# A Flamingo block on one core: k copied by VectorE, attention rows normalised by GpSimd, and a feed-forward that begins with half steps

## What is computed

```python
query = einsum("bnc,dc->bnd", ctx, Wq) + bq        # ctx: 4 x 256 x 128, f32
key = einsum("bnc,dc->bnd", ctx, Wk) + bk
attention = softmax(query @ key^T, axis=-1)        # 4 x 256 x 256
x = x + tanh(g_xattn) * einsum("bln,bmn->blm", layernorm(x), attention)
h = layernorm(x)                                   # then fp8
act = gelu(h @ w_gating[0]) * (h @ w_gating[1])    # 256 -> 1024, fp8 products
x = x + tanh(g_ffn) * (act @ w_linear)             # 1024 -> 256
```

## Time and profile before

| | |
|---|---|
| median of three runs | 50.8 us (50.74 to 51.58) |
| the profiled execution | 50.57 us |
| its span, first to last instruction | 48.8 us |
| TensorE busy | 42.9 us, 88% |
| VectorE busy | 35.7 us, 73% |
| ScalarE busy | 29.5 us, 60% |
| GpSimd busy | 16.9 us, 35% |

### The profile page before, as it was taken

The page is one execution under the profiler, slowest core; times in us unless marked ns, Lnnn a source line. Parts: engine busy times, 40 slices in busy tenths (PEclk is TensorE's granted clock), DMA queues, the critical chain, the costliest instruction groups (busy, mean ns, idle before and its releaser), DMA issues.

```text
span 48.8 us, 842 instructions
## 1 busy us (share of the span) xinstructions
PE 42.9 (88%) x245; PEld 29.6 (61%) x245; DVE 35.7 (73%) x111; ACT 29.5 (60%) x67; POOL 16.9 (35%) x35
## 2 busy tenths in 40 slices
PE   0999999995999999998999999999999999995300
PEld 0318788882887988863435655765656788872000
DVE  2101069999978979989999991887666998899910
ACT  4601643799799699844599749754446944662000
POOL 3205992009999823410510160000000697005000
PEclk9999999999999999999999999999999999999996
DMA  0495999999999991000000000000000025230083
GB/s 0 80 309 108 349 402 327 196 202 176 194 201 153 104 97 9 0 0 7 0 0 0 13 0 0 0 0 0 7 0 0 0 104 163 66 110 0 0 321 109
DMA packets 3460, 4.64 MB, mean 95 GB/s; under 512 B 384, under 2 KB 2048, under 8 KB 3456
## 3 DMA queue, kind: packets, MB, share of 16 engines
q1 hardware_dynamic: 2592, 3.80, 23.7%
q0 software_dynamic: 864, 0.79, 17.5%
HBM read 5.90 MB, written 1.05 MB: 142 GB/s over the span
## 4 chain that ended last, share of the span: by engine, by line
PE 64%; DVE 15%; DMA 9%; SPq 3%; ACT 2%; issue 1%; DVEq 1%
PE bank L627 15%; PE bank L633 14%; PE bank L652 14%; PE bank L587 14%; DMA x_sb<-x 9%; DVE st L403 6%; PE bank L559 4%; SPq L205 3%; DVE nmax L410 2%; PE bank L609 2%; DVE mv L406 2%; PE bank L552 2%; DVE aq L470 2%; DVE attn L421 1%; ACT xq L337 1%
## 5 line engine op out<-in xcount | busy, mean ns | idle before, releaser
L461 DVE SCALAR_TENSOR_TENSOR ap<-bank,gl 128x512 f16<-128x512 f32 (+1 forms) x20 | 11.6, 580 | 3.5 <-issue 1.6
L346 ACT ACTIVATE gl<-bank 128x512 bf16<-128x512 f32 (+1 forms) x20 | 10.0, 509 | 6.0 <-PE bank L627 6.0
L652 PE MATMUL bank<-wl,aq 128*128 128x256 fp8e4 x64 | 10.1, 273 | 0.7 <-DVE aq L470 0.6
L627 PE MATMUL bank<-xq,wg 128*128 128x512 fp8e4 (+1 forms) x40 | 10.2, 337 | 0.2 <-ACT xq L337 0.2
L633 PE MATMUL bank<-xq,wg 128*128 128x512 fp8e4 (+1 forms) x40 | 10.2, 337 | 0.0
L652 PEld LDWEIGHTS bank<-wl,aq 128*128 128x128 f16 x64 | 6.0, 98 | 4.1 <-DVE aq L470 1.6
L587 PE MATMUL bank<-attnT,xT_sb 128*128 128x256 f32 x32 | 8.1, 385 | 0.0
L470 DVE TENSOR_SCALAR aq<-ap 128x512 uint16<-128x512 uint16 (+1 forms) x20 | 6.6, 334 | 0.0
L270 POOL TENSOR_TENSOR yo<-ys,x 128x256 f32<-128x256 f32 x4 | 2.9, 750 | 9.3 <-ACT ys L354 9.3
L587 PEld LDWEIGHTS bank<-attnT,xT_sb 128*128 128x128 f32 x32 | 5.6, 190 | 0.7 <-ACT attnT L320 0.2
L255 POOL TENSOR_TENSOR r<-ve,neg_half 128x2 f32<-128x2 f32 x4 | 3.0, 760 | 8.5 <-DVE ve L444 8.5
(11 more groups left out here) (51 smaller groups left out, 55.9 us busy)
## 6 DMA issues: line engine op xcount, KB each, us to landing
x_sb<-x SPq DMA_DIRECT2D x4, 256.0 KB, 4.7
xT_sb<-xT SPq DMA_DIRECT2D x4, 256.0 KB, 8.5
out<-yo SPq DMA_DIRECT2D x6, 128.0 KB, 2.1
wg<-w_gating POOLq DMA_DIRECT2D x4, 128.0 KB, 10.1
par<-params_ctxT SPq DMA_DIRECT2D x1, 258.0 KB, 2.8
par<-params_ctxT SPq DMA_DIRECT2D x1, 256.0 KB, 4.2
wl<-w_linear POOLq DMA_DIRECT2D x2, 128.0 KB, 9.7
out<-yo SPq DMA_DIRECT2D x1, 256.0 KB, 2.0
```

Of the source, the lines that this page charges most:

```text
L346: nc.scalar.activation(gl[:, s % 2, toks], gate_b[s % 2][:, toks], ACT.Gelu_apprx_tanh).then_inc(gelu_ready, 1)
L461: nc.vector.scalar_tensor_tensor(ap[:, s % NAP, toks], up_b[s % 2][:, toks], ACT_SCALE, gl[:, s % 2, toks], ALU.mult, ALU.mult).then_inc(p ...
L627: mm = nc.tensor.matmul(gate_b[s % 2][:, toks], wg8[:, c, k, 0, o:o + P], xq[:, g, k, toks], start=(k == 0), stop=(k == KC - 1))
L652: mm = nc.tensor.matmul(halves(y_b[g][i])[:, t], aq[:, s % NAQ, m:m + P], wl8[:, j], start=(j == 0 and t == 0), stop=(j == HT - 1), skip_g ...
```

## The change

Four things move. VectorE copies k out of PSUM in place of ScalarE. GpSimd normalises the rows of all four sequences, and VectorE none. VectorE's program is reordered: stats1 of one sequence stands after each copy of k instead of three of them standing at the front. TensorE transposes the attention rows and xh tile by tile, with a wait for each tile of 128 rows, and its order of attend parts and of energy(0) and project_k(1) is shifted. The first two hidden slices of group 0 are made as half steps, sequence 0 first (two steps), then sequence 1 (two steps), which makes 22 steps of what were 20, with X_AFTER moved accordingly; turn_x2(1) now stands behind the two half steps of sequence 0.

```diff
-    STEPS = [divmod(n, HT) + (0, GB) for n in range(G * HT - SPLIT)]
+    FIRST = 2
+
+
+    STEPS = [(0, j, i, i + 1) for i in range(GB) for j in range(FIRST)]
+    STEPS += [divmod(n, HT) + (0, GB) for n in range(FIRST, G * HT - SPLIT)]
     STEPS += [(G - 1, j, i, i + 1) for i in range(GB) for j in range(HT - SPLIT, HT)]
     S = len(STEPS)
-    X_AFTER = (3, 6)
+    X_AFTER = (5, 8)
...
+            normalise(0)
+            normalise(1)
             scales1()
             shift_x(0)
+            normalise(2)
             shift_x(1)
-            normalise(B - 1)
+            normalise(3)
...
-            def k_out(b):
-                act.wait_ge(k_done, b + 1)
-                nc.scalar.activation(kT[:, b * L:(b + 1) * L], k_b[b % 2][:, 0:L], ACT.Identity,
-                                     bias=bk).then_inc(k_ready, 1)
...
             q_out(0)
-            k_out(0)
             q_out(1)
-            k_out(1)
             q_out(2)
-            k_out(2)
             exps(0)
             q_out(3)
-            k_out(3)
             exps(1)
             attn_out(0)
             exps(2)
+            attn_out(1)
             exps(3)
-            attn_out(1)
             attn_out(2)
...
+            def k_out(b):
+                dve.wait_ge(k_done, b + 1)
+                if b == 0:
+                    dve.wait_ge(s_ctx[0], 16)
+                nc.vector.tensor_scalar(kT[:, b * L:(b + 1) * L], k_b[b % 2][:, 0:L], bk, None,
+                                        ALU.add).then_inc(k_ready, 1)
...
-            def normalise(b):
-                invert_sum(b)
-                dve.wait_ge(rsum_ready, b + 1)
-                for t in range(LT):
-                    nc.vector.tensor_scalar(attn[:, b, t], e[:, b, t], rsum[:, b, t:t + 1], None,
-                                            ALU.mult).then_inc(attn_ready, 1)
...
-            for b in range(B - 1):
-                stats1(b)
+            k_out(0)
+            stats1(0)
             row_max(0)
-            stats1(B - 1)
+            k_out(1)
+            k_out(2)
+            stats1(1)
+            invert_sum(0)
             row_max(1)
-            normalise(0)
+            k_out(3)
+            stats1(2)
+            invert_sum(1)
             row_max(2)
-            normalise(1)
+            stats1(3)
             row_max(3)
-            normalise(2)
-            invert_sum(B - 1)
+            invert_sum(2)
+            invert_sum(3)
...
-                if b < B - 1:
-                    pe.wait_ge(attn_ready, LT * (b + 1))
-                else:
-                    pe.wait_ge(pool_attn_ready, LT)
...
-                turn(turn_b[b % 2], attn[:, b]).then_inc(attn_turned, 1)
+                for t in range(LT):
+                    pe.wait_ge(pool_attn_ready, LT * b + t + 1)
+                    for k in range(KC):
+                        mm = nc.tensor.transpose(halves(turn_b[b % 2])[:, k, t * P:(t + 1) * P],
+                                                 attn[:, b, t, k * P:(k + 1) * P], ident[:, :])
+                mm.then_inc(attn_turned, 1)
...
-                for k in range(KC):
-                    for t in range(LT):
+                for t in range(LT):
+                    if b < 2:
+                        pe.wait_ge(xh_ready, LT * b + t + 1)
+                    else:
+                        pe.wait_ge(act_xh_ready, LT * (b - 2) + t + 1)
+                    for k in range(KC):
...
-                    pe.wait_ge(xq_ready, GB * (g + 1))
+                    pe.wait_ge(xq_ready, GB * g + i1)
...
             project_k(0)
             project_q(1)
+            energy(0)
             project_k(1)
-            energy(0)
             project_q(2)
             project_k(2)
             energy(1)
...
             attend(0, [(0, 0), (0, 1)])
             turn_attention(1)
             attend(0, [(1, 0), (1, 1)])
+            attend(1, [(0, 0), (0, 1)])
             turn_attention(2)
-            attend(1)
+            attend(1, [(1, 0), (1, 1)])
+            attend(2, [(0, 0), (0, 1)])
             turn_attention(3)
-            attend(2)
+            attend(2, [(1, 0), (1, 1)])
             attend(3, [(0, 0), (0, 1)])
             turn_x2(0)
-            attend(3, [(1, 0)])
+            attend(3, [(1, 0), (1, 1)])
+            for s in range(FIRST):
+                ffn1(s)
             turn_x2(1)
-            attend(3, [(1, 1)])
             for s in range(S):
-                ffn1(s)
+                if s >= FIRST:
+                    ffn1(s)
                 if s >= LAG:
```

More of the change, by code:

```diff
@@ L157, in flamingo_block @@
         rsum_ready = sem("rsum_ready")
-        attn_ready = sem("attn_ready")
         pool_attn_ready = sem("pool_attn_ready")
@@ L192, in flamingo_block @@
         s_out = sem("s_out")
+        first_of_g1 = next(s for s, step in enumerate(STEPS) if step[0] == 1)
         def last_step(b):
@@ L388, in _ @@
                     xq_out(3)
-                if s == HT + LAG:
+                if s == first_of_g1 + LAG:
                     scale_out(0)
-                if s == HT + LAG + 1:
+                if s == first_of_g1 + LAG + 1:
                     scale_out(1)
@@ L554, in energy @@
                 mm.then_inc(energy_done, 1)
-            def turn(to, src):
-                for k in range(KC):
-                    for t in range(LT):
-                        mm = nc.tensor.transpose(halves(to)[:, k, t * P:(t + 1) * P],
-                                                 src[:, t, k * P:(k + 1) * P], ident[:, :])
-                return mm
             def turn_attention(b):
@@ L593, in turn_x2 @@
                 if b < 2:
-                    pe.wait_ge(xh_ready, LT * (b + 1))
-                else:
-                    pe.wait_ge(act_xh_ready, LT * (b - 1))
-                if b < 2:
                     pe.wait_ge(attnT_ready, B - 1 + b)
@@ L644, in ffn2 @@
                     pe.wait_ge(x2_ready, LT * B)
-                    pe.wait_ge(xq_ready, 2)
-                if s == HT:
+                if (g, j) == (0, 0):
+                    pe.wait_ge(xq_ready, i1)
+                if s == first_of_g1:
                     pe.wait_ge(xq_ready, B)
```

## The result

| | before | changed |
|---|---|---|
| median | 50.77 us (50.74 to 51.58, 4 runs) | 55.34 us (55.31 to 55.68, 4 runs) |
| ratio | | 1.090, 95% interval 1.085 to 1.095 |
| the profiled execution | 50.57 us | 55.35 us |
| its span | 48.8 us | 53.6 us |
| mean granted clock | 0.992 | 0.968 |

A forecast was written before the change was run, and what follows sets the result against it. TensorE was taken to bound the kernel: holes added, 2.85 + 0.24 + 0.5 + 1.1 + 0.18 + 0.24 = 5.1, less 1.42 removed, put 3.7 on 50.57, giving 54.3. Own range 53.0 to 54.9, overall 52.4 to 56.6.

The forecast's parts named there:

- The wait at turn_attention(2): On TensorE ahead of the third transposition: stands from 15.75 to 18.60 for GpSimd's rows of sequence 2, 2.85.
- the chain from the last statistics to the first xs: On GpSimd, from the last statistics to the first shifted x: takes 3.43 as before, of which the power is 1.68.
- three half blocks more: On TensorE ahead of turn_attention(2): listed as work without a wait, up to 15.75.
- Why scales1 is late: On GpSimd: it starts at 13.73 because VectorE's extra work makes the last statistics 3.1 late.
- second rival: VectorE's statistics complete by 11.2, so TensorE never stands at turn_attention(2): time 50.7, chance 0.10.
- first rival: Clock falls in TensorE's hole at turn_attention(2), delaying the feed-forward by 1.5 to 2.5: 55.8 to 56.8, chance 0.25.
- the forecast's hole of 0.5: On TensorE ahead of attend(3): waits for ScalarE's copy attnT(3) until 22.82, 0.5.
- The hole for gelu(0): On TensorE after sequence 0's half steps: waits for gelu(0) behind xq_out(1), 1.1, then product(0), 0.18.
- The wait for product(2): On TensorE in the feed-forward: product(2) stands behind sequence 3's second statistics on VectorE, 0.24.
- What was costed at nothing: Extra half steps, tile-wise waits, ScalarE's lost copies (1.9), VectorE's lost normalisations (2.3) and unmoved weight transfers: no effect on the time.
- The 0.45 that VectorE no longer loses: VectorE's normalisations beside GpSimd's xs: some 0.45 comes back, but VectorE is not waited for, so no gain.
- The sum: Whole kernel: 50.57 for the profiled execution and 3.7 of delay give 54.3.

The follow-up runs named there:

- e2: Changed kernel with stats1(3) ahead of row_max(2) on VectorE: 54.00 us, ratio 1.061.
- e11: Kernel before with only the rows moved: GpSimd normalises all four sequences in the changed kernel's order, ScalarE still copies k: 54.18 us, ratio 1.066.
- e9: Changed kernel with full steps from the start and stats1(3) ahead of row_max(2): 52.97 us, ratio 1.042.
- e1: Changed kernel with ten matmuls on zeros filling TensorE's hole ahead of turn_attention(2)'s wait for the rows: 54.23 us, ratio 1.070.
- e3: Changed kernel with GpSimd's normalise(2) ahead of scales1: 57.27 us.
- e4: Changed kernel with gelu(0) and gelu(1) ahead of xq_out(1) on ScalarE: 53.89 us, ratio 1.061.
- e5: Kernel before with only the half steps, turn_x2(1) behind the two of sequence 0: 51.77 us, ratio 1.022.
- e6: Changed kernel with full steps from the start and turn_x2(1) between the last quarters of attend(3), as before: 54.05 us.
- e7: Kernel before with only the transpositions of attention rows and xh tile by tile: 50.66 us, ratio 0.995.

## Why the prediction was right, and where it was not

**The wait at turn_attention(2).** Right, and close: statistics over at 13.64 (13.73 forecast), first shifted x at 16.82 (17.16), transposition at 18.37 (18.60). The copy of k on VectorE takes 0.48 and starts its successor after 0.40 (0.38 taken). A term that is off is the chain from the last statistics to the first xs, 3.18 instead of 3.43. TensorE is also through with the work ahead at 15.93 and not 15.75, so the hole is 2.44 from start to start, where the text had 2.85. Its list of that work is one half block too long ("three half blocks more"; with the block times given, 15.75 holds two, and two stand in the program), which did not enter the sum.

**Why scales1 is late.** Half right. In the changed kernel the row says that scales1 waited for the statistics, 0.53, and e2 gained that. But the text gave all of the delay to VectorE's extra work, and named statistics complete by 11.2 as the point from which TensorE never stands. e11 has them at 10.5, and the hole is 2.40. The rows of sequences 0 and 1 ahead of scales1, which wait for exps(1) in e11 and for the reciprocal behind stats1(2) in e2, hold it until 13.3 to 13.7 alone; VectorE's work holds it to about the same moment, so each hides the other. My second rival, "the statistics come in time", rested on a condition that does not suffice. In numbers: rows alone 54.2, copies of k alone 52.6, both 54.05 (full steps in all three). These are not pure differences: the kernel of the copies alone has stats1(3) early, and its partner in that is e9 with 52.97, so that there the rows on GpSimd add 0.4; and the kernel of the rows alone keeps TensorE's old order, with all of attend(1) behind the third transposition.

**The clock.** It was the first rival, with a chance of 0.25, that came true, not the forecast. I had priced it at 1.5 to 2.5 more; it cost 1.05 (e1). What I had right is that a part hides behind attnT(3): the forecast's hole of 0.5 there is missing in the changed kernel and is back, at 0.35, as soon as the clock stays up. The price was too high because I let every matmul of attend(1), attend(2) and turn_attention(3) behind the hole take twice its time, 2.9 more (3.0 by the text's own block times), and took off about 0.5 for what hides. The clock was low from 19.4 to 22.8 only: the first two matmuls of what was left of attend(1) and the last half block of attend(2), which starts at 22.86, ran at full rate. Against the filled hole the low clock added 1.6 (22.86, when the last half of attend(2) starts, is 9.05 behind scales1, against 21.44 or 7.46), and 0.54 of it hid behind attnT(3). This is the term that was mis-sized: with 1.05 instead of 1.5 to 2.5 the first rival gives 55.35, and 55.34 was measured. The measured time lies neither in the forecast's own range (53.0 to 54.9) nor in the first rival's (55.8 to 56.8), but between them; that it is inside 52.4 to 56.6 is owed to the width that the rival gave. The Trainium skill (TensorE: Matmul & The Clock Gate, Part 1) has the fall after idleness, which this trace agrees with, and e3 as well. The trace of e11, with a longer wait (2.40), has no fall.

**The hole for gelu(0).** Right: 1.05 and 0.26 (1.1 and 0.18 forecast). e4 shows that ScalarE's order is part of its cause: with gelu(0) ahead, 0.69 of the hole is left, for the transposition and the copy of sequence 1, which come late with the half steps. e5 shows the same 1.05 with the half steps alone, on the kernel before. The wait for product(2), 0.24 in the forecast, is 0.13. The prediction did not say outright that the half steps are a loss by themselves, though its own sum had it: 0.42 saved, about 1.5 added. e5 and e6 put it at 1.0 and 1.3.

**What was costed at nothing** stayed so. The tile-wise waits are worth 0.5% (e7). ScalarE's relief let exps(0) start at 8.69 instead of 9.86 and exps(1) at 10.79 instead of 11.48, but the third transposition waited for neither, and ScalarE waited more itself (5.1 for the transpositions, 0.8 before). The new places of energy(0), project_k(1) and the parts of attend were not run by themselves. The 0.45 that VectorE no longer loses beside GpSimd's xs is not waited for, as forecast.

**The sum.** Forecast 3.7 after 50.57; in the trace 4.8. Of the 1.1 between them the clock is 1.05.

## What to carry to other kernels

An engine with idle time is not free if its program has a shared step in it: ask what a new instruction ahead of that step waits for, because the step then waits for it too, and price that before moving it. Whether the rows of sequence 1 behind scales1 would have done better was not run. When two moves load the same chain, try each alone, since a single row names only what came last and hides the one that came just before. Smaller first steps start sooner, but they also cover less of the latency behind them; compare the matmul time that stands ahead of the first consumer with the time until its result is back.

## What the runs showed that I had not expected

In the changed kernel the clock did not fall in the hole but a microsecond behind it: TensorE was idle from 16.2 to 18.3 and resumed at full rate, the fall came at 19.4, and it took 3.4 us until the rate was back. A hole is thus not always paid for once it is over. The place of the fall is not fixed: it came 0.8 behind the resumption in e6, just at the resumption in e4 and within the hole of 3.14 in e3, and the clock stayed low for 3.4, 3.4 and 6.8.

Nor does the length of the hole alone decide, since the same kernel goes both ways. With a wait of 2.2 in the trace, the clock fell in all four executions of the changed kernel, in three of four of e6 and in one of four of e4; with 2.40 (e11) in one of four, and with 1.53 (e2, e9) in one of four each. What decides it no run here tells. So the 1.05 is the price of a fall and not of a hole, and the times of such a kernel can lie about 1 apart from one execution to the next.

The power on GpSimd costs 0.76 for two columns and 1.67 for eight, and a multiplication of the same eight columns 0.20: about 0.15 for each further column. It was the longest single step of the chain.
